# A recommendation tower: the first macro tile's table selections done tile by tile, with products between them

## The reference, cut to what matters

```python
# B = 2048 rows, 26 tables of width 128; ten tables of 1000 rows, the others have 1250 to 125000
e = stack([tbl_f[ids[:, f]] for f in range(26)], axis=1)          # (2048, 26, 128)
combined = concatenate([dense[:, None, :], e], axis=1)            # (2048, 27, 128)
inter = einsum('bfd,bgd->bfg', combined, combined)[:, iu, ju]     # 351 pairs, f < g
z = concatenate([dense, inter, dense], axis=1)                    # (2048, 607)
h = maximum(z @ W_top1 + b_top1, 0)                               # 512
h = maximum(h @ W_top2 + b_top2, 0)                               # 256
y = h @ W_top3                                                    # (2048, 1)
```

## Time and profile before

| | us |
|---|---|
| median of 3 runs (434.28 to 438.62) | 437.5 |
| the profiled execution's own time | 435.75 |
| its span, first to last instruction | 433.9 |
| TensorE busy | 395.5 |
| VectorE busy | 292.0 |
| POOL busy | 297.1 |

### The profile page before, as it was taken

How to read it: one execution, slowest core, us unless ns; L and a number is a source line. 1 busy time by engine, 2 the same in 40 slices (tenths; PEclk the granted TensorE clock), 3 DMA queues, 4 the chain that set the end, 5 groups by cost and what they waited for, 6 DMA issues and landing times.

```text
span 433.9 us, 8713 instructions
## 1 busy us (share of the span) xinstructions
PE 395.5 (91%) x3384; PEld 378.2 (87%) x3384; DVE 292.0 (67%) x445; ACT 242.8 (56%) x558; POOL 297.1 (68%) x263
## 2 busy tenths in 40 slices
PE   1866797699999999999999999999999999998997
PEld 1766687698999899998999899998999899988976
DVE  3999554887667866677677866677667866644241
ACT  3432665467463845577463845577463845579562
POOL 0788777687778677787778877787778877762000
PEclk9999998899999999999999999999999999999999
DMA  7997243222423144321333144221522134110000
GB/s 186 257 253 217 67 87 95 54 75 53 107 73 80 51 70 106 82 62 50 104 74 80 51 75 108 78 65 50 112 74 79 50 76 96 45 50 20 0 2 0
DMA packets 24608, 35.92 MB, mean 83 GB/s; under 512 B 6296, under 2 KB 18720, under 8 KB 24568
## 3 DMA queue, kind: packets, MB, share of 16 engines
q1 hardware_dynamic: 16376, 18.57, 19.0%
q0 software_dynamic: 8192, 16.79, 15.0%
HBM read 35.33 MB, written 0.01 MB: 81 GB/s over the span
## 4 chain that ended last, share of the span: by engine, by line
PE 74%; DVE 14%; ACT 5%; issue 4%; DMA 3%; SPq 0%; POOL 0%; DVEq 0%; ACTq 0%
PE gram_ps L418 22%; PE x_ps L399 14%; PE x_ps L400 13%; DVE hot L875 9%; PE x_ps L382 5%; PE tail_ps L459 5%; PE tail_ps L460 5%; PE tail_ps L461 5%; PE tail_ps L451 2%; DVE pairs L854 2%; DMA rows<-in_tbl_dram,ids_sb 2%; ACT x L638 2%; ACT pairs L638 1%; PE tail_ps L494 1%; DMA x<-in_tbl_dram 1%
## 5 line engine op out<-in xcount | busy, mean ns | idle before, releaser
L348 POOL DMA_INDIRECT rows<-in_tbl_dram,ids_sb x256 | 296.3, 1157 | 96.0 <-issue 46.1
L875 DVE TENSOR_TENSOR hot<-ids_all,row_f 125x1024 fp32r<-125x1024 int32 x160 | 189.0, 1221 | 51.8 <-PE x_ps L400 48.1
L399 PE MATMUL x_ps<-hot,table_hi 125*128 125x256 f32 x640 | 163.9, 293 | 28.1 <-DVE hot L875 16.3
L400 PE MATMUL x_ps<-hot,table_lo 125*128 125x256 f32 x640 | 157.9, 283 | 0.0
L399 PEld LDWEIGHTS x_ps<-hot,table_hi 125*128 125x128 f32 x640 | 123.1, 192 | 33.0 <-issue 23.0
L400 PEld LDWEIGHTS x_ps<-hot,table_lo 125*128 125x128 f32 x640 | 123.2, 192 | 0.0
L418 PE MATMUL gram_ps<-x 128*108 128x108 f32 x1024 | 109.7, 261 | 1.5 <-issue 0.6
L418 PEld LDWEIGHTS gram_ps<-x 128*108 128x108 f32 x1024 | 104.2, 177 | 2.9 <-issue 0.8
L638 ACT ACTIVATE picked<-x_ps 128x256 f32<-128x256 f32 x80 | 30.7, 383 | 88.2 <-PE x_ps L400 88.0
L638 ACT ACTIVATE gram<-gram_ps 44x208 f32<-44x208 f32 (+3 forms) x136 | 46.0, 338 | 30.7 <-PE gram_ps L418 27.2
L854 DVE COPY gram<-gram_ps 44x208 f32<-44x208 f32 (+1 forms) x120 | 44.3, 369 | 16.6 <-PE gram_ps L418 13.1
(11 more groups left out here) (74 smaller groups left out, 340.5 us busy)
## 6 DMA issues: line engine op xcount, KB each, us to landing
ids_all<-in_selected_ids_dram SPq DMA_DIRECT2D x80, 128.0 KB, 5.0
rows<-in_tbl_dram,ids_sb POOLq DMA_INDIRECT x256, 2.7
x<-in_tbl_dram SPq DMA_DIRECT2D x6, 448.0 KB
stage<-in_tbl_dram SPq DMA_DIRECT2D x3, 448.0 KB
rows<-in_r_dense_features_dram SPq DMA_DIRECT2D x16, 64.0 KB, 1.9
stage<-in_W_pairs_dram SPq DMA_DIRECT2D x1, 702.0 KB
stage<-in_W_dense_dram SPq DMA_DIRECT2D x2, 256.0 KB
stage<-in_W_dram SPq DMA_DIRECT2D x1, 512.0 KB
```

Of the source, the lines that this page charges most:

```text
L348: pool.indirect_dma_start(out=rows[t][:, slot, :], out_offset=None, in_=tables[GATHERED[slot - 1]], in_offset=bass.IndirectOffsetOnAxis(ap ...
L399: first = pe.matmul(bank, table_hi[j][:, c, :], v, start=(c == 0), stop=False)
L400: last = pe.matmul(bank, table_lo[j][:, c, :], v, start=False, stop=(c == VC - 1))
L875: dve.tensor_tensor(hot[h][:], ids_all[0:VK, j % IDS, :].unsqueeze(1).broadcast_to([VK, HALF, MACRO]), row_f[0:VK, these].unsqueeze(2).bro ...
```

## The change

For macro tile 0 alone, selections are done for one tile of 128 rows at a time (`select_first`): again 16 matmuls for each table, now of 128 columns each. Called a *half selection* below; there are 20, where there were ten full ones. One `hot` buffer now holds all 8 chunks for 128 rows, so one comparison of 125x1024 serves a half selection. The half selections of tile 0 run as the tables come in, those of tile 1 stand between the row groups and products of tile 0, and the full selections for macro tile 1 stand between the products of tile 1, the last four with nothing between.

All ten tables are loaded at once, each to the place that its low part takes later (`raws` lies over `table_lo`), with no waits; the ids of macro tile 0 come as four loads of five tables by one tile; POOL's start comes after three tables; its gathers of macro tile 0 wait for no count; the row numbers for the comparisons of macro tiles 0 and 1 are read from PSUM (`row_start`); the weights are loaded when the ids are. From macro tile 1 on, the order is what it was.

```diff
+    X_FIRST = ([("first", j, 0) for j in range(7)] + [("rows", 0, 0), ("first", 7, 0), ("first", 8, 0), ("rows", 0, 1),
+                ("first", 9, 0), ("rows", 0, 2), ("first", 0, 1), ("rows", 0, 3), ("first", 1, 1), ("rows", 0, 4)]
+               + [("first", j, 1) for j in range(2, 6)] + [("rows", 1, 0), ("first", 6, 1), ("first", 7, 1),
+                ("rows", 1, 1), ("first", 8, 1), ("first", 9, 1), ("rows", 1, 2), ("table", 0), ("rows", 1, 3),
+                ("table", 1), ("rows", 1, 4)] + [("table", j) for j in range(2, NS)]
+               + [("next rows", 0, g) for g in range(EARLY)])
...
     def pace_of(m, number):
 
+        if m == 0:
+            return 0
...
         table_hi = [sb(f"table_hi{j}", [VK, VC, D], F32R) for j in range(NS)]
+        with nc.sbuf_tensor("raws", [VK, NS, VC, D], F32) as raws:
+            pass
         table_lo = [sb(f"table_lo{j}", [VK, VC, D], F32R) for j in range(NS)]
...
+        table_raw = [raws[:, j] for j in range(NS)]
+        hot_first = [hot[i][:].rearrange("k c b -> k (c b)").rearrange("k (c b) -> k c b", c=VC) for i in range(HOTS)]
+        ids_first = ids_all[:].rearrange("p j b -> p (j b)").rearrange("p (j b) -> p j b", j=NS)
...
+        row_start = tail_ps[1][:, 0:VC]
...
+            def load_ids_first(part, t):
+
+                these = slice(part * IDS, (part + 1) * IDS)
+                src = selected_ids[these, t * P:(t + 1) * P]
+                sp.dma_start(ids_first[:, these, :], src.partition_broadcast(P)).then_inc(ids_first_loaded[part], 16)
 
             load_ids(0, TILES, ids_loaded[0])
-            for j in range(RAWS):
-                if j < IDS:
-                    load_ids_all(0, j)
+            load_ids_first(0, 0)
+            load_table(0)
+            load_table(1)
+            load_table(2)
+            sp.sem_inc(loads_begun, 1)
+            load_ids_first(1, 0)
+            load_dense(0, 0)
+            for j in range(3, NS):
                 load_table(j)
-            sp.sem_inc(loads_begun, 1)
-            for t in range(TILES):
-                load_dense(0, t)
+            load_dense(0, 1)
             load_ids(TILES, B // P, ids_loaded[1])
-            for j in range(IDS, NS):
-                if IDS < j <= IDS + NS - RAWS:
-                    load_table(RAWS + j - IDS - 1)
-                sp.wait_ge(hot_ready, 2 * (j - IDS + 1))
-                load_ids_all(0, j)
+            for part in range(2):
+                sp.wait_ge(hot_ready, first_number((part + 1) * IDS - 1, 0) + 1)
+                load_ids_first(part, 1)
             load_weights()
...
+            def select_first(j, t):
+
+                pe.wait_ge(hi_ready, j + 1)
+                pe.wait_ge(lo_ready, j + 1)
+                bank = x_bank(x_at(0, "first", j, t))[:, 0, :]
+                number = first_number(j, t)
+                pe.wait_ge(hot_ready, number + 1)
+                for c in range(VC):
+                    v = hot_first[number % HOTS][:, c, :]
+                    pe.matmul(bank, table_hi[j][:, c, :], v, start=(c == 0), stop=False)
+                    last = pe.matmul(bank, table_lo[j][:, c, :], v, start=False, stop=(c == VC - 1))
+                last.then_inc(x_filled, 1)
...
+            def first_tile():
+
+                for j in range(7):
+                    select_first(j, 0)
+                pe.wait_ge(ident_ready, 2)
+                transposes(0, 0, 0)
+                select_first(7, 0)
+                select_first(8, 0)
+                transposes(0, 0, 1)
+                select_first(9, 0)
+                transposes(0, 0, 2)
+                select_first(0, 1)
+                transposes(0, 0, 3)
+                select_first(1, 1)
+                transposes(0, 0, 4)
+                select_first(2, 1)
+                gram_products(0, 0, 0)
+                select_first(3, 1)
+                gram_products(0, 0, 1)
+                select_first(4, 1)
+                select_first(5, 1)
+                gram_products(0, 0, 2)
+                transposes(0, 1, 0)
+                select_first(6, 1)
+                gram_products(0, 0, 3)
+                select_first(7, 1)
+                transposes(0, 1, 1)
+                select_first(8, 1)
+                select_first(9, 1)
+                transposes(0, 1, 2)
+                select(0, 0)
+                transposes(0, 1, 3)
+                select(0, 1)
+                transposes(0, 1, 4)
+                select(0, 2)
+                gram_products(0, 1, 0)
+                select(0, 3)
+                gram_products(0, 1, 1)
+                select(0, 4)
+                gram_products(0, 1, 2)
+                select(0, 5)
+                gram_products(0, 1, 3)
+                for j in range(6, NS):
+                    select(0, j)
+                transposes(1, 0, 0)
+                transposes(1, 0, 1)
...
+            def pick_first(j, t):
+                at = x_at(0, "first", j, t)
+                bank = at % 2
+                act.wait_ge(x_filled, at + 1)
+                copy(picked[:, j, t * P:(t + 1) * P], x_ps[bank][:, 0, :]).then_inc(x_moved[bank], 1)
...
+            def build_first(j, t):
+
+                dve.wait_ge(ids_first_loaded[j // IDS], 16 * (t + 1))
+                number = first_number(j, t)
+                compare_ids(number, hot_first[number % HOTS], ids_first[0:VK, j, :], row_start[0:VK])
...
+            def first_tile():
+                build_first(0, 0)
+                split_table(0)
+                for j in range(1, NS):
+                    split_table(j)
+                    build_first(j, 0)
+                for j in range(NS):
+                    build_first(j, 1)
+                for j in range(4):
+                    build_hot(1, j)
+                keep_dense(0)
+                build_hot(1, 4)
+                gram_products(0, UNITS + 1)
+                build_hot(1, 5)
+                split_weights()
+                for j in range(6, NS):
+                    build_hot(1, j)
```

## The result

The changed kernel takes 470.01 us (median of 6 runs, 469.05 to 472.76), the kernel before 437.12 us in the same comparison (6 runs, 434.28 to 438.72): the ratio is 1.076, with a 95% interval of 1.071 to 1.081. Slower was forecast with a chance of 0.79. But 461 us was forecast, with a range that ends at 466, so the forecast of the time failed. The profiled execution after took 469.77 us, its span 468.0 us, 34.1 us more than before. My mark, the first full selection of macro tile 1, moved from 94.51 us to 128.51 us, by 34.0 us: all of the loss lies ahead of the mark, and 25.4 us of it were forecast.

The account below looks back on a forecast made before the run. TensorE, busy 91% of the span, was taken as the bound, though it waits for DVE in the opening. The steps put the mark at 119.9 us against 94.51, 25.4 us more: 435.75 + 25.4 = 461 us, range 438 to 466.

Parts of the forecast that it names:

- Items 1 and 2: Opening loads: extra ids cost 0.8 us, first half selection starts at 10.4 us, last table is in at 32 us.
- Rival D: Opening: short ids pieces keep tables from coming faster; low clock covers 12 us, early clock rise adds 2-4; within remaining 0.02.
- Rival A: Opening: the clock rises early and loads bound it; mark at 101.6 us, 443 us in all; chance 0.20.
- item 4: Opening on TensorE at low clock: 13 half selections of 3.45 us and five row groups; first unit at 58.9 us.
- C: Half selections: 128 float32r columns cost like float32, 3.6 us each at full clock; 470 us; chance 0.05.
- Item 5: Getting warm: first unit 2.8 us, half selection 3.45, second unit about 2.2 with the clock rising in it; ends 67.4 us.
- Item 6: Remaining six half selections at 1.9 us each, two units 3.1 us, three row groups 1.3 us; ends at 83.2 us.
- B: Half selections: weight load is no floor, 16 matmuls take 1.0 us, kernel gets faster, 432 us; chance 0.13.
- Item 7: Ten full selections, with a 3.8 us stall for the weight split and 1.0 us for the clock's fall; ends 115.8 us.
- Item 8: Before the mark: last copy, join and row copies on ACT take 3.1 us, as before; mark at 119.9 us.
- Item 9: Gathers, row numbers in PSUM and weight loads in the opening and macro tile 0: priced at nothing.
- my case: Low clock in the opening until units come in, half selections 1.9 us at full clock: 456 to 465 us; chance 0.50.

Follow-up runs that it names:

- e2_ids_long: Changed kernel with macro tile 0's ids laid out so each load reads 128 pieces of 2560 bytes instead of 640 of 512: 461.31 us, ratio 1.057.
- e1_wide: Changed kernel with each half-selection matmul streaming 256 columns instead of 128, the extra results unread: 457.78 us, ratio 1.049.
- before_narrow: Kernel before with its ten opening selections done as 32 matmuls of 128 columns each: ratios 1.067 and 1.075 in two comparisons on other chips.
- g5_wide_ids_split: Changed kernel with 256-column half-selection matmuls, ids in 2560-byte pieces and the weights split earlier, on DVE in four pieces: 440.97 us, ratio 1.008.
- g7_rows_sbuf: Changed kernel with its row numbers read from SBUF throughout instead of PSUM: 470.73 us, ratio 1.078.
- e4_wide_ids: Changed kernel with both 256-column half-selection matmuls and ids in 2560-byte pieces: 445.71 us, ratio 1.021.

## Why the forecast of the direction was right and that of the time wrong

**Items 1 and 2, the loads, are the step that failed.** I priced the ids by their bytes, at the rate at which whole tables stream: 0.8 us, with the first half selection at 10.4 us and no later wait for a table. It started at 16.86 us, 6.5 us later, and TensorE then waited 3.65 us for the fourth table. That is 10.1 us, and the first unit was late by 69.19 less 58.9, 10.3 us. e2_ids_long gives 9.4 us of it back, with the first unit at 59.78 us: same bytes, long pieces, the first half selection at 11.38 us, the time 461.31 us, the ratio 1.057 instead of 1.076. Rival D named the mechanism. Its price was wrong twice: "covered at the low clock" is true of the late tables, but not of the first one, for which nothing is there to cover, nor of a gap of 8.7 us between two; and the 2 to 4 us under A were 12.1 us. The row that could have warned me is in the page of before, among the DMA issues (count, size, median us to landing):

```profile
ids_all<-in_selected_ids_dram SPq DMA_DIRECT2D x80, 128.0 KB, 5.0
```

An ids load of 128 pieces of 1024 bytes took 5.0 us, 26 GB/s. Bytes over the rate of a full queue are only the lower bound for such a load; the other end, an estimate by this row, is 12.5 us for 320 KB at 26 GB/s. Measured: 11.0 us. The row is a rough one: in the page after, the loads of the same form show 3.2 us, by which 320 KB would be 8 us.

The Trainium skill, "DMA: Bandwidth & Descriptors", section "Specifications", puts the smallest transfer for line rate at 512 bytes. The pieces here are just that, and for this load the trace doesn't agree: 39 GB/s, at 0.28 of the engines' time.

**The clock, item 4: right.** Half selections ran at 0.21 us a matmul, 3.4 to 3.5 us each against 3.45, for 52 us, however full the queue was (the fourth to the seventh stand back to back from 30.98 to 44.91 us, 3.5 us each). A row group took 0.87 us. e1_wide and before_narrow show it from both sides: the same 16 matmuls of a selection with 256 columns got the opening to the full pace, and with 128 columns 320 in a row did not. Rival A fell by this, C by the 1.82 us at full clock. The level itself is inferred from the pace, since the granted clock reads 1.00 there. That C's time, 470 us, is what was measured is chance.

**Item 5**, getting warm: from the first unit to the end of the second 8.5 us were forecast, 6.7 passed (69.19 to 75.87): the rise came within the half selection, not in the second unit. That is 1.8 us to the good.

**Item 6**: the floor of the weight load was right in kind, 0.114 us a matmul where 0.117 was taken, and B fell. 15.8 us were forecast and 15.5 passed. The Trainium skill's 81 ns at 128 columns ("TensorE: Matmul & The Clock Gate", section "Back-to-back issue gap") is not reached with these float32r weights.

**Item 7**: ten full selections and the clock's fall were forecast at 32.6 + 1.0, and 33.9 us passed (91.37 to 125.26). The stall was 3.52 us against 3.8. Behind it some 16 matmuls start 0.21 us apart instead of 0.12, 1.5 us more, where 1.0 had been taken. g5_wide_ids_split shows the price of both together, 4.7 us. **Item 8**: 3.25 us against 3.1.

**Item 9**, at nothing: held for the gathers, the weights and the row numbers (g7_rows_sbuf).

The sum in marks: +10.3 from the loads, -1.8 from getting warm, and +0.1 from the rest give +8.6 us, 128.51 less 119.9. The range ended at 466 because D stood beside my case at no price.

What the change could give at best can be estimated. At full clock 20 half selections cost 20 x 1.82, 36 us, where ten full ones cost 20: 16 us more for the same products. In the opening of before the ten took 33.4 us, from 9.63 to 43.00 us, so TensorE had idled or run at the low pace for only 13 us of it. In the opening a mend of clock or loads can make no more than that good; e4_wide_ids and g5_wide_ids_split, which end up slower than before, fit it.

## What to carry to other kernels

To split a product by its columns need not split its cost: here 16 matmuls of 128 columns took 1.82 us at full clock, 16 of 256 columns about 2.0, and while little but matmuls of 128 columns ran the pace stayed low, for 52 us and 68 us. Price a load by the row of a load whose pieces are most like it, not by bytes over the best rate, and ask what stands behind it in the same queue. What the very first load costs is covered by nothing: there is no work yet to hide it.

## What the hardware showed that I had not expected

- Ids loads of 640 pieces of 512 bytes landed after 11.0 us (median of four), and SP's next six issues took 8.76 us; with 128 pieces of 2560 bytes 7.3 and 3.33 us. The DMA engines' share in the first 10 us was 0.28 and 0.79.
- The window rows give the granted clock as 1.00 for the opening, in which each matmul takes 0.21 us, the pace of the stretches that show 0.50. The pace is to be read from the starts.
- Many gathers took 0.94 us each in the opening after, and 1.96 us in that of before. The place of the row numbers explains little of it: 36.1 against 39.0 us for 32 gathers. DVE was busy for 26.2 us of the 50 between 10 and 60 us after, and for 40.8 before; that its work lengthens gathers is an inference, not tested.
